# Start order and placement of mask work in a two-stage graph layer (x and W_nb loaded first, low weights ahead of later statistics, first masks early, next masks late)

## The reference

```python
h = jnp.maximum(_layernorm(x, axis=-1), 0.0)
mask = (adj > 0).astype(x.dtype)
deg = jnp.sum(mask, axis=1, keepdims=True)
agg = mask @ h / jnp.maximum(deg, 1.0)
combined = jnp.concatenate([h @ W_self + b_self, agg @ W_nb + b_nb], axis=-1)
return x + jax.nn.relu(combined @ W_comb + b_comb)
```

## Time and profile before

| what | value |
|---|---|
| median of 3 runs | 913.62 us (911.9 to 917.82) |
| profiled execution | 915.82 us, its span 914.0 us |
| TensorE busy | 896.9 us, 98% of the span |
| VectorE busy | 799.1 us, 87% |
| ScalarE busy | 377.5 us, 41% |
| GpSimd busy | 91.0 us, 10% (only in the first stage) |
| granted TensorE clock | 0.997 in the mean |
| DMA | 312.80 MB, 342 GB/s in the mean |

### The profile page before, as it was taken

How to read it: one execution, slowest core, us unless ns; L and a number is a source line. 1 busy time by engine, 2 the same in 40 slices (tenths; PEclk the granted TensorE clock), 3 DMA queues, 4 the chain that set the end, 5 groups by cost and what they waited for, 6 DMA issues and landing times. The chain is left out here.

```text
span 914.0 us, 19105 instructions
## 1 busy us (share of the span) xinstructions
PE 896.9 (98%) x7720; PEld 760.1 (83%) x7720; DVE 799.1 (87%) x1512; ACT 377.5 (41%) x358; POOL 91.0 (10%) x132
## 2 busy tenths in 40 slices
PE   7999899899999999999999999999999999999997
PEld 5555478788888888888888888888888888888886
DVE  5999898898998988898889888888899998888884
ACT  3999854233333333332333333333333333333320
POOL 2888820000000000000000000000000000000000
PEclk9999999999999999999999999999999999999999
DMA  6467769999999999999999999999999999999950
GB/s 213 162 220 274 265 233 391 400 370 388 376 384 377 378 380 377 373 370 368 367 380 377 389 392 370 381 365 364 358 374 372 380 386 379 369 376 376 398 211 22
DMA packets 61367, 312.80 MB, mean 342 GB/s; under 512 B 6880, under 2 KB 8032, under 8 KB 28512
## 3 DMA queue, kind: packets, MB, share of 16 engines
q1 hardware_dynamic: 60736, 311.06, 87.7%
q10 hardware_dynamic: 544, 0.52, 0.2%
HBM read 294.78 MB, written 16.78 MB: 341 GB/s over the span
## 5 line engine op out<-in xcount | busy, mean ns | idle before, releaser
L625 PE MATMUL banks<-t,operands 128*128 128x257 f16 x7168 | 786.5, 272 | 2.6 <-DVE work L757 2.6
L625 PEld LDWEIGHTS banks<-t,operands 128*128 128x128 fp8e4 x7168 | 698.3, 97 | 90.7 <-issue 2.8
L468 ACT ACTIVATE mask<-stage,few 128x2048 fp8e4<-128x2048 int32 x128 | 252.7, 1999 | 415.5 <-DVE turned L720 318.9
L705 DVE TENSOR_SCALAR mask<-stage 128x2048 uint8<-128x2048 int32 x128 | 154.5, 1226 | 5.8 <-DMA stage<-in_adj_dram 5.8
L565 PE MATMUL banks<-t,xh 128*128 128x512 f16 x384 | 89.3, 383 | 4.2 <-DVE t L698 3.1
L757 DVE TENSOR_TENSOR work<-banks,work 128x512 f32<-128x512 f32 x32 | 22.1, 692 | 74.8 <-ACT work L518 74.8
L734 DVE TENSOR_TENSOR operands<-turned,operands 128x1024 uint32<-128x1024 uint32 x64 | 78.4, 1225 | 8.8 <-DVE turned L720 0.5
L714 DVE STREAM_TRANSPOSE operands<-mask 128x512 uint32<-128x512 uint32 x128 | 83.1, 687 | 0.2 <-DVE t L693 0.2
L720 DVE STREAM_TRANSPOSE turned<-mask 128x512 uint32<-128x512 uint32 x128 | 80.8, 669 | 0.0
L736 DVE TENSOR_TENSOR operands<-turned,operands 128x1024 uint32<-128x1024 uint32 x64 | 78.2, 1222 | 0.0
L565 PEld LDWEIGHTS banks<-t,xh 128*128 128x128 f16 x384 | 37.7, 98 | 44.0 <-issue 4.6
(11 more groups left out here) (62 smaller groups left out, 391.4 us busy)
## 6 DMA issues: line engine op xcount, KB each, us to landing
stage<-in_adj_dram SPq DMA_DIRECT2D x256, 1024.0 KB, 8.5
out_dram<-operands SPq DMA_DIRECT2D x32, 256.0 KB, 2.8
xh<-in_x_dram SPq DMA_DIRECT2D x32, 256.0 KB, 9.5
own<-out_dram SPq DMA_DIRECT2D x32, 256.0 KB, 10.5
out_dram<-xh SPq DMA_DIRECT2D x32, 256.0 KB, 6.0
t<-in_x_dram SPq DMA_DIRECT2D x30, 256.0 KB, 4.4
turned<-in_x_dram SPq DMA_DIRECT2D x2, 256.0 KB, 5.4
t<-in_L_gnn_W_nb_dram ACTq DMA_DIRECT2D x1, 256.0 KB, 4.0
```

The source lines that it names most:

```text
L468: act.activation(mask[:, b, :].bitcast(FP8), stage[:, b, :], ACT.Sigmoid, bias=steep, scale=STEEP, saturate=False).then_inc(formed_s, 1)
L625: mm = pe.matmul(banks[:, n, 0:width], bytes_of[:, c, :, s], t16[:, KQ * h + SUB * c + s, SLOT[n], 0:width], start=(h == 0 and c == 0 and ...
L705: dve.tensor_scalar(mask[:, b, :], stage[:, b, :], 0.0, float(MINUS_ONE_BYTE), ALU.is_gt, ALU.mult).then_inc(formed_v, 1)
```

## The change

- Loads: x of pair 0, the two W_self and W_comb halves on SP, then x of pairs 1 and on; W_nb and its W_comb half on ScalarE's queue as before, and the two bias loads behind them.
- Pairs 0 and 1 become batches of their own. VectorE makes the statistics, shift and norm of pair 0, then the statistics of pair 1, and does the low half of W (`w_low(0)`) ahead of the statistics of pairs 2 and 3.
- GpSimd makes the four wide copies of the biases and the negated sum in two parts; TensorE does the b product before the transposes of pair 1. 20 instead of 16 warm transposes.
- adj of step 0 is loaded at pairs 0, 1, 3, 5 and formed at pairs 4, 7 (ScalarE), 9 and 13 (VectorE), with the transposes at 10 and 14.
- The own masks of step 1 are made after the first stage; the loads ahead are those of step 1 only (pairs 11, 15, 18, 21), and all four of step 2 follow after the first stage. `make_third(2)` stands ahead of the loop over r, where it was behind the first `merge_a` and `outer_sums`.

```diff
--- before.py
+++ after.py
@@ -24,7 +24,7 @@
 KQ = PAIRS // HALVES_OF_K
 DONE = 16
-WARM = 16
+WARM = 20
 MINUS_ONE_BYTE = 184
@@ -42,11 +42,11 @@
 RING = 3
-BATCHES = [(0, 2), (2, 4), (4, 6), (6, 8)] + [(p, p + 4) for p in range(8, PAIRS, 4)]
+BATCHES = [(0, 1), (1, 2), (2, 4), (4, 6), (6, 8)] + [(p, p + 4) for p in range(8, PAIRS, 4)]
 STATS_AHEAD = {0: (6, 7), 1: (8, 9), 2: (10, 11)}
-FINISHED_AT = {(0, 2)[b - 3] if b < 5 else BATCHES[b][1] - 10: b for b in range(3, len(BATCHES))}
-SHIFTED_AT = {0: 2, **{j + 1: b for j, b in FINISHED_AT.items()}}
+FINISHED_AT = {(0, 2)[b - 4] if b < 6 else BATCHES[b][1] - 10: b for b in range(4, len(BATCHES))}
+SHIFTED_AT = {0: 3, **{j + 1: b for j, b in FINISHED_AT.items()}}
 BATCH_OF = {p: b for b, (first, end) in enumerate(BATCHES) for p in range(first, end)}
@@ -76,17 +76,15 @@
 A22, A11, A12, A21 = range(4)
-FORM_STEPS_S = {20: A12, 22: A21}
-FORM_STEPS_V = {23: A22, 25: A11}
-TURN_STEPS_V = {24: A22, 26: A11}
+FORM_STEPS_S = {4: A12, 7: A21}
+FORM_STEPS_V = {9: A22, 13: A11}
+TURN_STEPS_V = {10: A22, 14: A11}
 TURN_STEPS = {30: (A12, A21)}
 DIFFERENCE_STEP = 31
-NEXT_STEPS_V = {27: A22, 28: A11}
-
 X_AHEAD = 14
-LOAD_STEPS = {12: A12, 14: A21, 16: A22, 18: A11}
-NEXT_LOADS = {21: (1, A12), 23: (1, A21), 24: (1, A22), 26: (1, A11), 28: (2, A22), 29: (2, A11)}
+LOAD_STEPS = {0: A12, 1: A21, 3: A22, 5: A11}
+NEXT_LOADS = {11: (1, A22), 15: (1, A11), 18: (1, A12), 21: (1, A21)}
 def norms_s(j):
@@ -331,13 +329,10 @@
                 sp.dma_start(out[r, :, :], x_again[:, r % 2, :]).then_inc(stored[r % 2], DONE)
             load_x(0)
-            load_x(1)
             sp.dma_start(ws_t, w_self_t.rearrange("(h p) n -> p h n", p=P)).then_inc(w_loaded[0], DONE)
             sp.dma_start(wc[:, 0:HALVES, :], w_comb[0:D, :].rearrange("(h p) n -> p h n", p=P)).then_inc(w_loaded[0], DONE)
-            load_x(2)
-            load_x(3)
-            sp.dma_start(b_cols, b_cols_in[:, :]).then_inc(b_loaded, DONE)
-            sp.dma_start(bc_row, b_comb.rearrange("(a n) -> a n", a=1).partition_broadcast(P)).then_inc(b_loaded, DONE)
+            for j in range(1, 4):
+                load_x(j)
             for j in range(4, X_AHEAD):
                 load_x(j)
@@ -356,8 +351,7 @@
             for n in range(RING):
                 sp.wait_ge(own_stored[n], len(range(n, PAIRS, RING)) * DONE)
             load_again(0)
-            load_block(2, A12)
-            load_block(2, A21)
+            load_step(2)
             load_step(3)
             load_again(1)
             for r in range(PAIRS):
@@ -410,10 +404,17 @@
                     pool.memset(t16[:, first:end, SLOT[n], D:D + 1], value).then_inc(ones_set, 1)
             root_of(0)
+            pool.wait_ge(b_loaded, 2 * DONE)
+            for m in range(2 * HALVES):
+                pool.tensor_copy(b_wide[:, m, :], b_cols[:, m:m + 1].to_broadcast([P, P])).then_inc(wide_ready, 1)
+            root_of(1)
+            pool.wait_ge(sum_high, 1)
+            pool.tensor_scalar(w12[:, 0, :, W_MINUS:W_WIDE], w12[:, 0, :, W_SUM:W_F1], -1.0, None, ALU.mult
+                               ).then_inc(sum_negated, 1)
             pool.wait_ge(sum_ready, 1)
-            pool.tensor_scalar(w12[:, :, :, W_MINUS:W_WIDE], w12[:, :, :, W_SUM:W_F1], -1.0, None, ALU.mult
+            pool.tensor_scalar(w12[:, 1, :, W_MINUS:W_WIDE], w12[:, 1, :, W_SUM:W_F1], -1.0, None, ALU.mult
                                ).then_inc(sum_negated, 1)
-            for b in range(1, 3):
+            for b in range(2, 4):
                 root_of(b)
             for j in range(PAIRS + 1):
@@ -478,24 +479,28 @@
             act.dma_start(wn_t, w_nb_t.rearrange("(h p) n -> p h n", p=P)).then_inc(w_loaded[1], DONE)
             act.dma_start(wc[:, HALVES:2 * HALVES, :], w_comb[D:2 * D, :].rearrange("(h p) n -> p h n", p=P)
                           ).then_inc(w_loaded[1], DONE)
+            act.dma_start(b_cols, b_cols_in[:, :]).then_inc(b_loaded, DONE)
+            act.dma_start(bc_row, b_comb.rearrange("(a n) -> a n", a=1).partition_broadcast(P)).then_inc(b_loaded, DONE)
             act.wait_ge(zeroed, 3)
             act.activation(rdeg[:, 0:1], steep, ACT.Sigmoid).then_inc(tables_ready, 1)
-            for j in range(2):
-                for t in norms_s(j):
-                    norm(j, t)
+            for t in norms_s(0):
+                norm(0, t)
             act.wait_ge(w_product, 1)
             act.activation(w_second, w_of(1)[:, :, 1, :], ACT.Copy, scale=W_SCALE).then_inc(second_copied, 1)
             w_high_half(1)
             sum_high_half()
             high_of_h(0)
+            for t in norms_s(1):
+                norm(1, t)
             act.wait_ge(w_product, 2)
             w_high_half(0)
+            high_of_h(1)
             for t in norms_s(2):
                 norm(2, t)
             for j in range(PAIRS + 2):
-                if j + 1 < PAIRS:
+                if 1 <= j < PAIRS - 1:
                     high_of_h(j + 1)
                 if j + 3 < PAIRS:
                     for t in norms_s(j + 3):
@@ -554,7 +559,7 @@
                 if j == 0:
                     pe.wait_ge(w_ready, 2)
                     pe.wait_ge(sum_ready, 1)
-                    pe.wait_ge(sum_negated, 1)
+                    pe.wait_ge(sum_negated, 2)
                 if j >= RING:
                     pe.wait_ge(evicted, j - RING + 1)
                 if j == 2:
@@ -577,13 +582,14 @@
                         mm = pe.matmul(pair_ps[1][:, n, kk * D:(kk + 1) * D], w_t[:, m, kk * P:(kk + 1) * P],
                                        wc[:, n * HALVES + m, :], start=(m == 0), stop=(m == HALVES - 1))
                 mm.then_inc(w_product, 1)
+                if j == 1:
+                    pe.wait_ge(wide_ready, 2 * HALVES)
+                    for m in range(2 * HALVES):
+                        mm = pe.matmul(pair_ps[2][:, 0, 0:D], b_wide[:, m, :], wc[:, m, :],
+                                       start=(m == 0), stop=(m == 2 * HALVES - 1))
+                    mm.then_inc(c_product, 1)
                 turn(j)
             project(0)
-            pe.wait_ge(wide_ready, 2 * HALVES)
-            for m in range(2 * HALVES):
-                mm = pe.matmul(pair_ps[2][:, 0, 0:D], b_wide[:, m, :], wc[:, m, :],
-                               start=(m == 0), stop=(m == 2 * HALVES - 1))
-            mm.then_inc(c_product, 1)
             turn(2)
             for j in range(1, PAIRS):
                 if j + 2 < PAIRS:
@@ -830,12 +836,11 @@
                 dve.scalar_tensor_tensor(x_blocks(r, 0, 3), own_blocks(r, 0, 3), 0.0, x_blocks(r, 0, 3), ALU.max, ALU.add
                                          ).then_inc(out_ready, 1)
-            for p in range(2):
-                stats_of(p)
+            stats_of(0)
             shifts(0)
-            for j in range(2):
-                for t in norms_v(j):
-                    norm(j, t)
+            for t in norms_v(0):
+                norm(0, t)
+            stats_of(1)
             dve.wait_ge(second_copied, 1)
             dve.wait_ge(w_high, 1)
@@ -844,20 +849,21 @@
             dve.wait_ge(sum_high, 1)
             dve.tensor_tensor(w12[:, 1, :, W_SUM:W_F1], w_sum, w12[:, 0, :, W_SUM:W_F1], ALU.subtract).then_inc(sum_ready, 1)
             low_of_h(0)
-            for p in range(2, 4):
-                stats_of(p)
+            shifts(1)
+            for t in norms_v(1):
+                norm(1, t)
             w_low(0)
-            shifts(1)
+            stats_of(2)
+            stats_of(3)
+            low_of_h(1)
+            stats_of(4)
+            shifts(2)
             for t in norms_v(2):
                 norm(2, t)
-            dve.wait_ge(b_loaded, 2 * DONE)
-            for m in range(2 * HALVES):
-                dve.tensor_copy(b_wide[:, m, :], b_cols[:, m:m + 1].to_broadcast([P, P])).then_inc(wide_ready, 1)
-            for p in range(4, 6):
-                stats_of(p)
+            stats_of(5)
             for j in range(PAIRS + 3):
-                if j + 1 < PAIRS:
+                if 1 <= j < PAIRS - 1:
                     low_of_h(j + 1)
                 if j + 3 < PAIRS:
                     for t in norms_v(j + 3):
@@ -876,8 +882,6 @@
                     form(0, FORM_STEPS_V[j])
                 if j in TURN_STEPS_V:
                     turn_own(0, TURN_STEPS_V[j])
-                if j in NEXT_STEPS_V:
-                    form(1, NEXT_STEPS_V[j])
                 if j in TURN_STEPS:
                     dve.wait_ge(h_turned, PAIRS)
                     for b in TURN_STEPS[j]:
@@ -889,16 +893,18 @@
                 dve.wait_ge(own_stored[n], len(range(n, PAIRS, RING)) * DONE)
             dve.wait_ge(combined, PAIRS)
             dve.wait_ge(t_low, 2 * PAIRS)
-            make_second(1)
+            form(1, A22)
+            turn_own(1, A22)
+            form(1, A11)
+            turn_own(1, A11)
             make_third(1)
             make_first(2)
             make_second(2)
+            make_third(2)
```

(2 more changed lines are left out.)

## The result

The changed kernel takes 920.6 us as the median of 7 runs, before takes 913.56 (8 runs beside them): the ratio is 1.007, with a 95% interval of 1.0052 to 1.0089. So it is 5 to 8 us slower, inside the 1% for which I gave 0.95, but outside my range of 909.8 to 917.0, and with the wrong sign.

What follows compares the result with a forecast made beforehand. TensorE's second-stage matmuls (786.5 us) end the kernel, so only that stage's beginning and its 2.57 us stall could move the end. Start -0.3, first masks -0.1, next masks 0: 913.2 us from 913.62, range 909.8 to 917.0.

Steps and rivals of the forecast that it cites:

- The start: Up to projection 2: begins near 25.4 instead of 25.74, a gain of 0.3 us.
- the fall between projections 0 and 1: TensorE idle some 3 us there; where the clock falls, projection 1 takes 4.15 for 2.75, losing 1.4 us.
- the low half of W ends at 15.0: VectorE in the start: the later of two branches, 14.1 and 15.0; before it was 15.73.
- The first masks: Step 0's masks at pairs 4 to 14: 4.5 us of new stalls against 4.6 at the old place, difference -0.1.
- The remaining 13 statistics pairs cost 0.4: First stage after the early masks: VectorE at 3.06 us per pair against TensorE's 3.03, 0.4 us in all.
- the 4.1 us up to pair 15: First stage: a stall of 0.2 from ScalarE's masks, then VectorE's own 3.9 us falling on TensorE whole.
- The rival that VectorE regains its lead: First stage: VectorE speeds up when late, the 3.9 us are mostly absorbed, giving 909.5; chance 0.2.
- The next masks and the second stage: Masks made after the first stage: a new 1.7 us stall at step 2, out of the old 2.57; net 0.
- landing minus 17.3: Second stage: stall before merge_a(0) is step 2's last block landing minus 17.3, from stage beginning; decides beyond 19.9.
- the landing term: Second stage: step 2's last adj block lands near 19 us after the stage begins, bounds 18 and 23.
- the rival of the slower supply: Second stage: step 2's last block lands later than 19.9; at 23 it costs 3.1 net, 916.3; chance 0.2.
- the new stall would come out of the old one: Second stage: the 1.7 us at step 2 is taken from the old 2.57 us stall, TensorE resuming at 51.87.

Runs made afterwards that it cites:

- e0: The kernel before, run once more with no edit: 914.5 us, ratio 1.0004.
- e1: Kernel before with only the start changed (load order, own batches for pairs 0 and 1, warm transposes, wide copies on GpSimd): 917.46 us, ratio 1.0032.
- e4: Changed kernel with 5 and 10 unused matmuls in TensorE's idle times between projections 0 and 1: 919.5 us, ratio 1.0042 to the kernel before.
- e14: e4 with 20 unused matmuls of 256 columns ahead of step 2 of the second stage: 917.97 us, ratio 1.0039 to the kernel before.
- e5: Changed kernel with GpSimd's norm of pair 3 ahead of the root of pairs 4 and 5: 918.5 us, ratio 1.0029 to the kernel before.
- e11: e10 with the changed kernel's start, but GpSimd's norms of pairs 3 and 4 each ahead of the root that follows: 914.34 us, ratio 1.0008.
- e7: Kernel before with only ScalarE's two masks of step 0 and their loads moved early, to pairs 4 and 7: 916.38 us, ratio 1.0018.
- e8: Kernel before with only VectorE's two masks of step 0, their transposes and loads moved early (pairs 9, 10, 13, 14): 915.42 us, ratio 1.0009.
- e10: e9 with step 0's masks at pairs 18 and 26 (ScalarE), 25 and 28 (VectorE), and step 1's loads at 20 to 29: 913.7 us, ratio 0.9997.
- e2: Kernel before with only the masks of step 0 and their loads moved to the first pairs: 916.82 us, ratio 1.0029.
- e3: Kernel before with only the next masks moved behind the first stage, step 1's loads at pairs 21 to 26: 915.44 us, ratio 1.0005.
- e6: e3 with make_third(2) put back behind the first outer_sums: 915.21 us, ratio 1.0008 to the kernel before.
- e9: e6 with load_again(0) behind load_step(2) in SP's queue: 916.15 us, ratio 1.001 to the kernel before.
- e13: e11 with 18 unused matmuls of 256 columns ahead of step 4 of the second stage: 913.65 us, ratio 0.9995 to the kernel before.
- e12: Kernel before with 20 unused matmuls of 256 columns ahead of step 4 of the second stage: 914.39 us, ratio 1.0.

## Why the prediction was wrong

*The start* (forecast: 0.3 gained; 3.1 lost against e0, 2.4 against the trace that the forecast was made from). The step that failed is the clock: I named the fall between projections 0 and 1 and its price, 1.4, and left it out of the sum. It happened in both traces in which nothing filled that time, e1 and the changed kernel. From projection 0 to projection 2 the changed kernel took 13.0 us, e4 and e14 with the time filled 10.5: 2.5 us, and not 1.4, since the matmuls of projection 1 took 4.81 for 2.75 and the work ahead of them 0.4 more. (In e5 and e11 GpSimd's norm of pair 3 came earlier, that wait of TensorE was gone, and the clock stayed up too.) The rest, 0.7 against e0, stays with the clock up (e14, projection 2 at 25.74): the new order brought nothing there. The base failed too: in the profiled execution of before the first product took 3.78 us. So it did in e7 and e8, and 3.70 in e10, and in these four projection 2 began at 25.55 to 25.86; in e0, e2, e3, e6 and e9, with the same start, the product took 1.99 and projection 2 began at 24.72 to 25.32. The forecast took the worse of two cases for the only one.

That the low half of W ends at 15.0, as forecast, is luck. The b_comb load landed 7.8 us after issue, at 10.1 rather than 8.9, and the four copies took 1.01, half of my value, so root 1 ended at 11.9 for 12.0; but that chain was not the one that decided, nor was the first W product, which ended at 8.5. VectorE waited until 9.35 for x of pair 1, now behind W_self and W_comb in SP's queue, and had no idle time from there to the norm of pair 1. VectorE's timeline of the changed kernel:

```profile
9.35 0.75 DVE L647 BATCH_NORM_STATS2 few<-t 128x6 f32<-128x256 f32 x2 [2.31 <-DMA t<-in_x_dram]
...
13.20 0.41 DVE L685 TENSOR_SCALAR t<-t,few 128x256 f32<-128x256 f32 x1
14.31 0.69 DVE L704 SCALAR_TENSOR_TENSOR t<-banks,t 128x512 f16<-128x512 f32 x1 [0.70 <-ACT t L473]
```

From 15.0 on the chain was right: 7.5 us forecast to projection 1, 8.0 measured, 0.4 of it by the lower clock.

*The first masks* (forecast: 4.5 of stalls for 4.6; measured 6.5 for 3.5). "The remaining 13 statistics pairs cost 0.4" is the step that failed. Lead lost is not refilled, that was right, and the 4.1 us up to pair 15 came out at 3.8 (0.98 + 0.26 + 0.19 + 0.82 + 1.39 + 0.12). That these agree is in part luck: ScalarE's masks were to cost 0.2 and cost 2.4 up to pair 16 when they stood alone (e7), and only the 0.82 begins with a wait for VectorE's low half, those at pairs 8 and 12 with one for GpSimd's norm. But then come 1.3, 0.7 and 0.7 at pairs 16, 20 and 24, 2.7 us for the 0.4, also with waits for GpSimd's norm behind its root, which I had costed at 1 for all and only as a possibility. The old place was overrated too: of its 4.6 us, 1.1 was a wait of that one execution. The rival that VectorE regains its lead (0.2) is refuted by e2, e7 and e8.

*The next masks and the second stage* (forecast 0; measured +0.35 against e0, e3 alone nothing). The mechanism held to its point of decision: the last block of step 2 was formed at 144.54, 20.4 after the stage began; the rule "landing minus 17.3" gives 3.1, measured 3.14, and beyond 19.9 it costs more than the old stall, here by 0.5. So the landing term, 19, was 1.4 too early, and it was the rival of the slower supply that came true, by 0.5. (Its upper bound in the sum, +3.5, does not follow from a landing at 23, which gives the 3.1 of the rivals.) VectorE's timeline of the changed kernel:

```profile
142.06 1.23 DVE L711 TENSOR_SCALAR mask<-stage 128x2048 uint8<-128x2048 int32 x1 [3.36 <-DMA stage<-in_adj_dram]
144.54 1.23 DVE L711 TENSOR_SCALAR mask<-stage 128x2048 uint8<-128x2048 int32 x1 [1.25 <-DMA stage<-in_adj_dram]
...
151.18 0.68 DVE L763 TENSOR_TENSOR work<-banks,work 128x512 f32<-128x512 f32 x1
```

That the new stall would come out of the old one was right: no second stall followed. That TensorE resumes at a fixed time after the stage's beginning was not. ScalarE's last form ahead of step 4, which waited for its block in each of them, began at 166.72 in e0, 167.55 in e8, 167.33 in e10 and 165.83 in e13, although their second stages began between 115.72 and 120.35.

*The range.* Its upper end took each bad case alone. Start and masks both went the bad way, 3.1 + 3.0, and the base was an execution 2.2 above its median.

*The signs.* Of those named for a right forecast, projection 1 near 22.5 came at 23.03, and the wait ahead of step 2 came at its place (24.7 after the stage's beginning) but as 3.14 for 1.7. Between 42 and 66 TensorE lost 3.6 us for some 4, mostly not to VectorE's low half; one stall was left between 92 and 115 (0.7 at pair 24), the first product took 2.16 and not 3.78, the second stage began at 124.13 and not by 120.5, and the smaller second wait was absent.

*What stays open.* The executions of before reach from 911.6 to 918.7. They go with the mean granted clock of each: of the 119 run beside e0 to e14, the 13 at 0.993 took 917.1 to 918.4, and of the 37 at 0.998 or more all but one took less than 914.8. The medians at 0.993 and 0.998 lie 4.6 us apart, as much as 0.005 of 914 us. Why the clock falls in one execution and not in another is open, and so is the spread within one value of it. Why the traces of e1, e2, e4 and e5 lose 1 to 3 us more than their first stages do is seen in them as a clock fall at the second stage's stall, but e12 does not show that preventing it helps the kernel before. No version here is faster than before beyond its interval.

## What to carry to other kernels

Where an engine has no spare time in a stretch, work put there costs what its lead does not cover, and its cost does not end with it: every later chain that relied on the lead (here variance, root, norm, transpose, once per four pairs) pays until the engine has spare time again. Before moving work, look for the stretch with slack, not for the one with an earlier time stamp. Idle time of TensorE is dearer than it is long when a slow stretch follows: a term that is named with its price belongs in the sum. And a gain ahead of a stage that is set by its supply is worth only what the supply lets through: e13 began the second stage 2.3 us earlier and its step 4 0.9 earlier.

## What the runs showed of the hardware

The first product ran at full speed after nothing but transposes in most traces. In e0 sixteen of them were followed, 1.24 us later, by a product of 1.99, in the changed kernel twenty by one of 2.16. (The granted clock of the stretches reads 1.00 there in all of them, also where the product took 3.78, so here the durations tell it.) Of the nine traces with sixteen transposes the product took 1.99 in five and 3.70 to 3.78 in four (rows 3, e7, e8, e10); of the seven with twenty it took 1.99 to 2.44 in all. The Trainium skill, TensorE: Matmul & The Clock Gate, section Part 4: PE-mode transpose, has it that transposes do not count towards the faster clock; these rows disagree. Whether the extra four help is not shown: none of seven beside four of nine is too few to tell, and no run changed their number alone.

The fall in the start, behind waits of 1.22 and 2.42 us, cost about what the slow instructions took over: 2.06 in projection 1 and 0.4 ahead of it, 2.5 in all. Waits in the second stage, 2.0 to 3.3 us, were followed by the lower clock, or saw it fall, in e1, e2, e4, e5, e6, e10 and e11 and not in before, e0, e3, e7, e9 and the changed kernel. GpSimd's root took 0.70 for 2 columns, 1.04 for 4 and 2.04 for 8, at 128 partitions; by the timeline above that growth is what makes a batch of four pairs dear.
